# Rope in a two-layer attention and mixture-of-experts kernel: the first 128 rows on VectorE alone, the second 128 rows on GpSimd and among the first attention steps

## What is computed

```python
def _apply_rope(x, sin, cos):
    xp = x.reshape(x.shape[:-1] + (x.shape[-1] // 2, 2))
    swapped = jnp.stack((-xp[..., 1], xp[..., 0]), axis=-1).reshape(x.shape)
    return x * cos + swapped * sin

q = _apply_rope(q, sin, cos)
k = _apply_rope(k, sin, cos)
scores = jnp.einsum('bhqk,bhsk->bhqs', q, k) / jnp.sqrt(jnp.asarray(dk, x.dtype))
scores = jnp.where(causal, -jnp.inf, scores)
attn = jax.nn.softmax(scores, axis=-1)
out = jnp.einsum('bhqs,bhsv->bqhv', attn, v).reshape(B, S, H * dk)

x = x + _layernorm(_L0_attn_ref(_layernorm(x), ...))
x = x + _layernorm(_L0_ffn_ref(_layernorm(x), ...))
x = x + _layernorm(_L1_attn_ref(_layernorm(x), ...))
x = x + _layernorm(_L1_ffn_ref(_layernorm(x), ...))
```

## Time and profile before

| | |
|---|---|
| median of 3 runs | 893.3 us (893.18 to 894.45) |
| time of the profiled execution | 893.29 us |
| its span, from the first to the last instruction | 891.5 us |
| PE busy | 722.0 us (81%) |
| DVE busy | 509.9 us (57%) |
| ACT busy | 343.2 us (38%) |
| POOL busy | 274.8 us (31%) |
| mean granted TensorE clock | 0.914 of full speed |

### The profile page before, as it was taken

How to read it: one execution, slowest core, us unless ns; L and a number is a source line. 1 busy time by engine, 2 the same in 40 slices (tenths; PEclk the granted TensorE clock), 3 DMA queues, 4 the chain that set the end, 5 groups by cost and what they waited for, 6 DMA issues and landing times. The chain is left out here.

```text
span 891.5 us, 14204 instructions
## 1 busy us (share of the span) xinstructions
PE 722.0 (81%) x4419; PEld 423.4 (47%) x4419; DVE 509.9 (57%) x1372; ACT 343.2 (38%) x724; POOL 274.8 (31%) x303
## 2 busy tenths in 40 slices
PE   4988999983799999999704768999982999999940
PEld 2533344242357777777502423334342646777720
DVE  3298779116834444555465999697317652354527
ACT  3624576833323333333204344556753310233311
POOL 1410111200046777776400441111110003377520
PEclk9999999996799999999956969999996799999975
DMA  3460110501228888987360360010002101377853
GB/s 91 129 202 15 61 30 2 190 1 47 70 65 258 265 264 278 282 268 238 121 226 0 101 202 29 14 68 33 1 1 104 48 1 26 103 254 253 266 174 108
DMA packets 63973, 109.00 MB, mean 122 GB/s; under 512 B 14953, under 2 KB 40705, under 8 KB 63793
## 3 DMA queue, kind: packets, MB, share of 16 engines
q1 hardware_dynamic: 54640, 94.25, 33.6%
q0 software_dynamic: 9216, 14.06, 4.6%
q10 hardware_dynamic: 64, 0.03, 0.0%
HBM read 84.89 MB, written 19.99 MB: 118 GB/s over the span
## 5 line engine op out<-in xcount | busy, mean ns | idle before, releaser
L1216 DVE TENSOR_REDUCE mx<-ps 128x1 f32<-128x512 f32 (+3 forms) x304 | 179.7, 656 | 45.3 <-PE ps L714 37.0
L1009 ACT ACTIVATE X<-ps 128x1024 f32<-128x1024 f32 (+1 forms) x192 | 146.0, 809 | 85.3 <-PE ps L740 84.8
L619 POOL DMA_INDIRECT KA<-token_rows,row_of_slot x96 | 98.3, 1024 | 161.0 <-DVE row_of_slot L1388 112.3
L897 PE MATMUL ps<-X,KA 128*128 128x128 f32 x1152 | 145.0, 276 | 1.5 <-DMA KA<-in_ex 1.0
L897 PEld LDWEIGHTS ps<-X,KA 128*128 128x128 f32 x1152 | 136.2, 192 | 3.1 <-DVE X L1451 1.5
L711 PE MATMUL ps<-KA,QA 112*128 112x512 bf16 (+3 forms) x384 | 113.8, 345 | 16.9 <-DVE mx L1216 8.5
L626 POOL DMA_INDIRECT outs<-X,token x96 | 97.1, 1011 | 67.1 <-issue 31.6
L606 POOL TENSOR_SCALAR_AFFINE_SELECT X<-X 128x512 f32<-128x512 f32 x64 | 40.6, 634 | 233.1 <-ACT X L1009 233.1
L1448 DVE TENSOR_TENSOR X<-ps,X 128x128 f32<-128x128 f32 x96 | 28.0, 292 | 129.0 <-ACT X L1097 129.0
L740 PE MATMUL ps<-QA,KA 114*128 114x512 bf16 (+3 forms) x384 | 92.7, 327 | 3.6 <-ACT X L1009 3.4
L658 PE MATMUL ps<-identf,xn 128*128 128x128 f32 x64 | 14.9, 424 | 83.0 <-ACT xn L943 66.0
(11 more groups left out here) (209 smaller groups left out, 879.3 us busy)
## 6 DMA issues: line engine op xcount, KB each, us to landing
KA<-in_ex SPq DMA_DIRECT2D x96, 512.0 KB
outs<-empty SPq DMA_DIRECT2D x4, 1024.0 KB, 7.6
KA<-in_dn SPq DMA_DIRECT2D x64, 64.0 KB
X<-outs SPq DMA_DIRECT2D x8, 512.0 KB, 6.0
V<-outs SPq DMA_DIRECT2D x8, 512.0 KB, 7.4
QA<-X SPq DMA_DIRECT2D x28, 128.0 KB, 2.5
KA<-X SPq DMA_DIRECT2D x28, 128.0 KB, 2.5
QA<-w_sdn SPq DMA_DIRECT2D x28, 128.0 KB, 2.5
```

Of the source, the lines that this page charges most:

```text
L619: pool.indirect_dma_start(out=rows[:, r, :], out_offset=None, in_=token_rows[L], in_offset=bass.IndirectOffsetOnAxis(ap=row_of_slot[L][:, ...
L897: mm = pe.matmul(ps[:, 2 + r % 2, m * P:(m + 1) * P], w_ex[:, w, col:col + P], rowsT[:, r % 2, k, :], start=(k == 0), stop=(k == KD - 1))
L1009: nc.scalar.activation(probs[:, st % PB, 2 * p:2 * p + 2, off:CH], ps[:, 4 + 2 * p:6 + 2 * p, off:CH], ACT.Exp, scale=SCALE).then_inc(S(f" ...
L1216: v.tensor_reduce(mx[:, part, i, h0:h0 + nh], ps[:, n % RB, 0:nh * w].rearrange("p (h w) -> p h w", h=nh), AX.X, ALU.max)\
```

## The change

In the second layer:

- Rope of the first 128 rows (`m` = 0) is made on DVE whole: shuffle, product with sine, product with cosine, sum.
- Of the second 128 rows (`m` = 1) DVE only turns the pairs, after its own subtractions, and signals `swapped`. POOL waits until DVE's last subtraction is done (`left2` of `m` = 0, K) and then makes the two products and the sum of Q and of K.
- `swapped` and `by_cos` move from V's memory to X's, where the probabilities come later.
- `split(1, 0)` on ACT stands behind the DMAs of group 0's first row maxima, ahead of the first exp. `split(1, 1)` stands behind the exps of step 0.
- POOL's second subtractions of `m` = 1 stand ahead of the masks of steps 1 and 2.
- V's padding is written by ACT, before the norm of the second attention's input; V's copies no longer wait for the rope.

In the first layer POOL writes V's padding at the start, ahead of its subtractions instead of behind them.

```diff
-        swapped = V[:, :, :, :].rearrange("p a b c -> p (a b c)")[:, 0:2 * T].rearrange("p (a t) -> p a t", a=2)
-        by_cos = V[:, :, :, :].rearrange("p a b c -> p (a b c)")[:, 2 * T:4 * T].rearrange("p (a t) -> p a t", a=2)
+        swapped = X[:, 0:2 * T].rearrange("p (a t) -> p a t", a=2)
+        by_cos = X[:, 2 * T:4 * T].rearrange("p (a t) -> p a t", a=2)
...
+                if L == 0:
+                    ch.link(pool.memset(V[:, :, :, DH + 1:], 0.0))
+                    pool.memset(V[:, :, :, DH:DH + 1], 1.0).then_inc(S("v_pad"), 1)
+                else:
+
+                    pool.wait_ge(*left(1, 0, 1, 2))
+                    for j in range(2):
+                        pool.wait_ge(S("qk_sb1"), (2 + j + 1) * NC)
+                        ch.step(pool.tensor_tensor(by_rows(by_cos[:, j, :]), qkf(1, j), by_rows(cos_t[:, :]), ALU.mult))
+                        pool.wait_ge(S("swapped"), j + 1)
+                        ch.link(pool.tensor_tensor(by_rows(swapped[:, j, :]), by_rows(swapped[:, j, :]),
+                                                   by_rows(sin_t[:, :]), ALU.mult))
+                        pool.tensor_tensor(qkf(1, j), by_rows(by_cos[:, j, :]), by_rows(swapped[:, j, :]), ALU.add)\
+                            .then_inc(S("roped"), 1)
+                for j in range(2):
+                    take_part(pool, L, 1, j, 1)
+                if L == 0:
+                    for j in range(2):
+                        take_part(pool, L, 1, j, 2)
...
+                    if L == 1 and st in (1, 2):
+
+                        take_part(pool, 1, 1, st - 1, 2)
...
-                        pe.wait_ge(S(f"v_pad{L}"), 1)
+                        pe.wait_ge(S("v_pad"), 1 + 2 * L)
...
+                if L == 1:
+                    act.wait_ge(S("summed0"), NC)
+                    nc.scalar.activation(V[:, :, :, DH + 1:].rearrange("p t h d -> p (t h) d"),
+                                         empty[:, 0:1].rearrange("p (a b) -> p a b", a=1)
+                                         .broadcast_to([P, NT * H, 32 - DH - 1]), ACT.Copy).then_inc(S("v_pad"), 1)
+                    nc.scalar.activation(V[:, :, :, DH:DH + 1].rearrange("p t h d -> p (t h d)"), ones[:, 0:NT * H], ACT.Copy)\
+                      .then_inc(S("v_pad"), 1)
...
-                split(1, 0)
-                split(1, 1)
-
-                if L == 1:
-                    act.wait_ge(S("roped"), 2 * KD)
+                if L == 0:
+                    split(1, 0)
+                    split(1, 1)
...
                     if x[0] == "score":
                         exps(*x[1:])
+                        if L == 1 and x[1:] == (0, 1):
+                            split(1, 1)
...
+                        if L == 1 and (g, c) == (0, 0):
+                            split(1, 0)
...
+                def turn_pairs(j, m):
+
+                    swap = [x ^ HG for x in range(32)]
+                    return v.stream_shuffle(by_rows(swapped[:, j, :]), qkf(m, j), swap)
+
+                if L == 1:
+                    dve.wait_ge(S("rope"), 32)
+                    for j in range(2):
+                        q, by_sin = qkf(0, j), by_rows(swapped[:, j, :])
+                        dve.wait_ge(S("qk_sb1"), (j + 1) * NC)
+                        ch.link(turn_pairs(j, 0))
+                        ch.step(v.tensor_tensor(by_sin, by_sin, by_rows(sin_t[:, :]), ALU.mult))
+                        ch.link(v.tensor_tensor(by_rows(by_cos[:, j, :]), q, by_rows(cos_t[:, :]), ALU.mult))
                         v.tensor_tensor(q, by_rows(by_cos[:, j, :]), by_sin, ALU.add).then_inc(S("roped"), 1)
+                for part in (1, 2):
+                    for j in range(2):
+                        take_part(dve, L, 0, j, part)
+                if L == 1:
+                    for j in range(2):
+                        dve.wait_ge(S("qk_sb1"), (2 + j + 1) * NC)
+                        turn_pairs(j, 1).then_inc(S("swapped"), 1)
```

More of the change, by code:

```diff
@@ L577, in _ @@
                     pool.wait_ge(S("e_down"), TILES[0])
-                for m in range(KD):
-                    if L == 1:
[L580 to L597, removed]
+                if L == 0:
[16 more added lines that the diff above has]
+                        take_part(pool, L, 1, j, 2)
                 for st in range(NG * NSTEP):
@@ L953, in _ @@
                     act.wait_ge(S("bias_qkv"), 32)
-                if L == 1:
-                    act.wait_ge(S("summed0"), NC)
                 def qk_out(m):
@@ L1188, in _ @@
                 xT_copy(f"a{L}")
-                for m in range(KD):
-                    for j in range(2 if L == 1 else 0):
-                        n = 2 * m + j
-                        q, by_sin = qkf(m, j), by_rows(swapped[:, j, :])
-                        dve.wait_ge(S(f"qk_sb{L}"), (n + 1) * NC)
-                        if n == 0:
-                            dve.wait_ge(S("rope"), 32)
-                        swap = [x ^ HG for x in range(32)]
-                        ch.link(v.stream_shuffle(by_sin, q, swap))
-                        ch.link(v.tensor_tensor(by_sin, by_sin, by_rows(sin_t[:, :]), ALU.mult))
-                        dve.wait_ge(S("by_cos"), n + 1)
-                        v.tensor_tensor(q, by_rows(by_cos[:, j, :]), by_sin, ALU.add).then_inc(S("roped"), 1)
-                    for part in (1, 2):
-                        for j in range(2):
-                            if (m, j) in DVE_PARTS:
-                                take_part(dve, L, m, j, part)
+                def turn_pairs(j, m):
[9 more added lines that the diff above has]
+                        ch.link(v.tensor_tensor(by_rows(by_cos[:, j, :]), q, by_rows(cos_t[:, :]), ALU.mult))
+                        v.tensor_tensor(q, by_rows(by_cos[:, j, :]), by_sin, ALU.add).then_inc(S("roped"), 1)
+                for part in (1, 2):
[5 more added lines that the diff above has]
+                        turn_pairs(j, 1).then_inc(S("swapped"), 1)
                 for x in UNITS:
```

## The result

| | before | after |
|---|---|---|
| median, 14 runs each | 893.15 us (889.19 to 895.74) | 885.3 us (882.63 to 889.29) |
| ratio, with its 95% interval | | 0.9914 (0.9896 to 0.9932) |
| profiled execution | 893.29 us | 885.09 us |
| its span | 891.5 us | 883.3 us |
| mean granted clock | 0.914 | 0.919 |

Faster, as forecast, by 7.8 us. The forecast was 6.1, its range ended at 885.5.

The account below looks back on a forecast made before the run. The end of nb, the negated maximum at the second attention's entry, was taken to set the schedule. Terms: -7.1 (entry) + 0.9 (splits) + 0.1 (first layer) = -6.1 us, from 893.3 to 887.2 us; range 885.5 to 890.4.

Parts of the forecast that it names:

- Rope on DVE: Second attention's entry: first 128 rows' rope on DVE alone takes 4.95 us per tensor, K done at 498.5.
- TensorE's start: First maxima start at 510.9, 0.35 us gained on SP's DMAs; wrong if it does not move while DVE idles.
- nb: Negated maximum on DVE at the attention's entry: 0.17 us instead of 3.04, ending at 518.7; wrong if stretched again.
- The entry and its end: Second attention's entry: nb ends 7.1 us earlier, 4.3 from earlier maxima and 2.9 from its wait for POOL.
- The six products on POOL: POOL's products and sums for the second rows' rope: 2.12 us each, one 2.36, from 504.7 to 517.7.
- the margin of 0.6: Time in us between the end of POOL's rope, 517.7, and nb's start, 518.3.
- The collision: Rival: POOL's rope ends after 518.3 and nb waits, costing 1.7 us, at most 2.1; 888.9 us, chance 0.17.
- The splits: ACT: first splits hidden before the first exp; second splits between exps of steps 0 and 1 cost 0.9 us.
- The padding on ACT: V's padding, 2.1 us on ACT before the norm, hidden in 5.03 us of idle time; costs nothing.
- The first layer: POOL's early memset of V delays DVE's first small operation; costs 0.1 us, bounds 0 and 0.45.
- everything behind the attention passed on one to one: Projection and everything behind it wait for the attention, so its end, 6 us earlier, carries through.
- the clock only as a rival in the attention's steps: Rival: TensorE's clock stays low for the steps' first 10 us, losing 6 us; 893.3 us, chance 0.07.

Follow-up runs that it names:

- after_d3: Changed kernel with three idle DVE products (3.8 us) between the projection's statistics and the scales, second layer; 888.18 us, ratio 0.9938 to before.
- after_d2: Changed kernel with two idle DVE products (2.5 us) between the projection's statistics and the scales, second layer; 888.85 us, ratio 0.9952 to before.
- after_copy: The changed kernel run again without any edit; 885.12 us, ratio 0.993 to before.
- pool_late: Changed kernel with POOL's rope starting only when DVE has turned both pairs; 882.16 us, one execution.
- split_late: Changed kernel with the second splits of rows 2 behind step 3's exps and POOL's last subtractions behind step 3's mask; 885.99 us, one execution.
- split_gaps: Changed kernel with Q's second split behind step 1's exps, K's behind step 2's, POOL's last subtractions ahead of masks 2 and 3; 886.52 us, ratio 0.9925 to before.
- before_hold: Kernel before with 66 and 76 unread matmuls filling TensorE's pauses behind the two layers' output projections; 884.92 us, ratio 0.992 to before.
- gaps_hold: split_gaps with 66 and 76 unread matmuls filling TensorE's pauses behind the output projections; 879.02 us, ratio 0.9853 to before.
- after_hold: Changed kernel with 66 and 76 unread matmuls filling TensorE's pauses behind the output projections; 881.16 us, ratio 0.9864 to before.
- the filled pair: before_hold and after_hold, the kernels before and after with TensorE's pauses filled by unread matmuls; 884.92 and 881.16 us.

## Why the prediction was right in kind and too small in size

**Rope on DVE: right.** All products and sums take 1.22 to 1.23, K is done 9.8 us behind the first shuffle, forecast 9.9.

**TensorE's start: right in most traces, and outside its bounds in the first.** Forecast 22.3 us behind the first shuffle; 22.7 in before. It was 23.06 in the first trace of the change, later than in before although DVE idled 5.86 us, which the forecast had named as a sign of being wrong. The other traces with the new rope fall in two groups: 22.97 and 23.00 in after_d3 and after_d2, 22.31 to 22.45 in the other eight. SP issues the last two DMAs into KA at the same distance in both groups (18.87 us behind the shuffle in after, 18.85 in after_copy), so they land later in the first; why is open.

**`nb`: right in size, and right by luck in its 0.17.** In the first trace it took 0.17 us and ended 30.8 us behind the shuffle, forecast 30.1; the 0.7 are the DMA's. In after_copy it took 0.48 and ended at 30.3: stretched again, if little, another of the forecast's signs. The entry and its end gave 6.51 in the first trace, and in after_copy 7.25, forecast 7.1.

**The six products on POOL: a term mis-sized.** I took 2.12 each and read the 2.36 of before as a product beside a shuffle. In the first trace they all take 2.34 to 2.36, most of them with no shuffle beside them. What differs is the input: those with two fp32 tiles take 2.35, those that subtract a bf16 part take 2.12, in the rows of before as well. With them POOL's rope ended 30.09 us behind the first shuffle in both unedited traces, forecast 29.1, and the margin of 0.6 was gone. Only where TensorE started late did `nb` find POOL idle, by 0.29 us; in after_copy it was ready at 29.64, met the last sum and took 0.48. In all it cost nothing that the stage shows (7.90 and 7.91). I had given the difference to the shuffle where the input types fitted the rows as well.

**The collision: it came, and its price was wrong.** I took "what POOL is late", 1.7 us. pool_late was 2.5 us late and lost 0.24. The price is what is left of the running instruction: between 0 and 2.3, by where `nb` falls in it (0.3 in after_copy), and more only where instructions follow without a gap, as the memset did in before.

**The splits: right.** Forecast 0.9, measured 0.78, and 0.77 gone in split_late and split_gaps. The padding on ACT (1.79 and 0.40 us, forecast 2.1) is covered: ACT still idles 3.02 ahead of the norm, as this row shows.

```profile
475.81 0.40 ACT L954 ACTIVATE V<-ones 128x128 f32<-128x128 bf16 x1
479.23 2.07 ACT L945 ACTIVATE xn<-xres,shift,rstd 128x256 f32<-128x256 f32 x4 [3.02 <-DVE shift L1155]
```

**The first layer: right, as far as it can be read.** The small operation at 6.45 took 0.34 instead of 0.17, behind POOL's memset; the chain there is 0.12 longer, forecast 0.1 (0.30 in split_late, within the bounds). Without added matmuls the first shuffle lies between 488.6 and 490.4 in the four traces with the old rope, and between 488.1 and 491.3 in the eight with the new one, so the 1.81 us of the first pair are no cost of the change that I could show. With them it is 485.53 in before_hold, 486.41 in gaps_hold and 488.23 in after_hold, so such a cost is not excluded either.

**What failed: everything behind the attention passed on one to one.** The forecast had the clock only as a rival in the attention's steps, and only as a loss. But the program has a second place where TensorE starts cold, behind the 17 us pause ahead of the router, and there its level is now the one and now the other. In the first pair of traces the router stage went from 45.78 to 42.11 us, in the second from 45.86 to 42.46: 3.7 and 3.4 us that the sum put at nothing, in code that the change leaves as it was. With the pause filled the stage is equal within 0.4 us in both kernels, so these microseconds are the clock's. They and the 5.8 to 6.5 of entry and attention are more than the 7.8 of the medians, as the traces are single executions.

How the 7.8 of the medians divide is less certain. The runs list a mean clock with each time. Of 70 runs of before, 9 have one of 0.916 or more; they average 889.9 us, the other 61 893.1. Of the 21 runs of the changed kernel (after and after_copy) 14 have 0.917 or more and average 884.3, the other 7 887.6. Between like groups lie 5.6 and 5.4 us; the larger share of the upper group, 0.67 instead of 0.13, at some 3.2 us, is worth 1.7. That this adds up to the 7.3 between the means is arithmetic, and the mean clock is no label of the router's level: the traced execution of split_gaps has 0.917 with a router of 6.88 us, that of after_d3 0.911 with 4.08. Nor do the times fall in order as the mean clock rises: before averages 891.6 at 0.910 (8 runs), 895.1 at 0.911 (7) and 892.1 at 0.914 (13). At 0.913, which both kernels have, the averages are 7.7 apart (9 runs and 4). So the split into some 5.5 for the forecast's mechanism and 1.7 for the clock is an estimate and not shown, and the filled pair, with its 3.8 us, does not confirm it. What decides the level stays open.

## What to carry to other kernels

Look for every place where TensorE starts behind a pause: its clock can win or lose 3 us there for a change that never touches the place, and filling the pause takes this out of the comparison. A small DVE operation on the critical path should have no long POOL instruction beside it, and above all no two back to back. Cost an operation by a row with the same input types, not by one with the same shape.

## What I had not expected of the hardware

- Matmuls that nobody reads, in two pauses, made the kernel before 7.0 us faster (884.92 against 891.92). All 76 took 16.57 us, and a pause of 0.60 was left; with 60 and a pause of 4.05 nothing was won.
- On POOL a product of two fp32 tiles of 128x1024 took 2.34 to 2.36 us, a subtraction of a bf16 from an fp32 tile 2.12.
- A wait of 0.08 us between two POOL instructions (518.30 to 518.38) was enough for DVE to get in; a product followed directly by a memset kept it out for 3.04.
- A maximum over PSUM was not held by any POOL instruction in these traces (6.13 to 6.22 us for 11 units in both kernels).
